# Two graph layers on one core: doubly buffered probabilities, the output written per head by VectorE, the probabilities' residual on GpSimd

## The reference

```python
# layer 0: W1 = W2 = adj
h = jnp.maximum(_layernorm(x), 0.0)
A = einsum('od,bdn->bon', adj, h);  C = A + b
x = x + max over the last axis of relu(A[:, :, None, :] + (C - A)[:, :, :, None])
# layer 1: masked attention, 8 heads of 64
h = jnp.maximum(_layernorm(x), 0.0)      # the kernel folds both norms into one h
q, k, v = h @ Wq + bq, h @ Wk + bk, h @ Wv + bv
scores = q k^T / 8 + (-1e9 where adj == 0)
x = x + softmax(scores) @ v
```

## Time and profile before

| | |
|---|---|
| median of 3 runs | 1403.61 us (1401.77 to 1403.91) |
| the profiled execution | 1401.24 us |
| its span, first to last instruction | 1399.4 us |
| mean granted clock of TensorE | 0.977 of full |
| PE busy | 1310.5 us, 94% |
| POOL busy | 1251.0 us, 89% |
| DVE busy | 1125.2 us, 80% |
| ACT busy | 878.7 us, 63% |
| chain that ended last | PE 55%, DMA 22% (nearly all probsT<-probs), DVE 15% |

### The profile page before, as it was taken

One profiled execution on the slowest core, in us unless ns is written; L12 is line 12 of the kernel. 1 busy time (PEld: TensorE's weight loads), 2 busy tenths in 40 slices (PEclk: granted clock), 3 DMA queues, 4 the chain that ended last, 5 costly groups with the idle time before them and its releaser, 6 DMA issues.

```text
span 1399.4 us, 32539 instructions
## 1 busy us (share of the span) xinstructions
PE 1310.5 (94%) x11145; PEld 657.2 (47%) x11145; DVE 1125.2 (80%) x1460; ACT 878.7 (63%) x1294; POOL 1251.0 (89%) x1288
## 2 busy tenths in 40 slices
PE   4899999999999999999999999999999999999962
PEld 1344444444444444454445444444444444444531
DVE  6468878888888788788898888888789888887874
ACT  4666666666666666666666666666666666666531
POOL 2889999999999999999999999999999999999721
PEclk8999999999999999999999999999999999999975
DMA  6235554555545545556455554655545556555534
GB/s 197 60 84 107 136 129 114 138 123 123 139 113 132 130 113 140 123 123 139 112 137 126 125 137 112 137 125 124 136 115 135 128 120 140 115 134 114 90 78 104
DMA packets 441372, 171.66 MB, mean 123 GB/s; under 512 B 406784, under 2 KB 406912, under 8 KB 441344
## 3 DMA queue, kind: packets, MB, share of 16 engines
q1 hardware_dynamic: 440000, 171.03, 52.7%
q10 hardware_dynamic: 1344, 0.27, 0.1%
HBM read 37.03 MB, written 33.55 MB: 50 GB/s over the span
## 4 chain that ended last, share of the span: by engine, by line
PE 55%; DMA 22%; DVE 15%; issue 4%; SPq 2%; ACT 1%; DVEq 0%; POOL 0%; POOLq 0%; ACTq 0%
PE proj L691 26%; DMA probsT<-probs 21%; PE proj L703 13%; PE o_ps L735 7%; DVE probs L495 7%; PE proj L676 6%; PE sc L720 4%; DVE attn L527 3%; SPq L239 2%; DVE a_max L481 1%; DVE out_scale L523 1%; DVE mean_var L474 1%; DVE inv_sum L521 1%; DMA x_in<-in_x 0%; SPq L219 0%
## 5 line engine op out<-in xcount | busy, mean ns | idle before, releaser
L691 PE MATMUL proj<-hT,w 128*128 128x512 f16 x3072 | 688.4, 381 | 11.5 <-DMA hT<-h 7.1
L691 PEld LDWEIGHTS proj<-hT,w 128*128 128x128 f16 x3072 | 291.0, 98 | 360.3 <-issue 16.8
L703 PE MATMUL proj<-w,hT 128*128 128x512 f16 x1536 | 352.4, 379 | 1.1 <-DVE w L579 1.1
L339 POOL TENSOR_TENSOR qkT<-qk,qkT 128x512 f16<-128x512 f32 x256 | 298.6, 1167 | 12.1 <-ACT qk L392 11.9
L407 ACT ACTIVATE probs<-shifted 128x1024 f16<-128x1024 f32 x128 | 135.3, 1057 | 193.7 <-DMA probsT<-probs 180.3
L390 ACT ACTIVATE qkT<-proj,bqk_up 128x512 f16<-128x512 f32 x256 | 173.4, 677 | 108.3 <-PE proj L691 108.3
L481 DVE TENSOR_REDUCE a_max<-proj 128x1 f32<-128x512 f32 x124 | 85.8, 692 | 191.5 <-PE proj L676 191.3
L327 POOL TENSOR_TENSOR xbv<-x_in,bv_rows 128x512 f32<-128x512 f32 x128 | 227.6, 1778 | 10.6 <-POOL y L318 2.2
L703 PEld LDWEIGHTS proj<-w,hT 128*128 128x128 f16 x1536 | 149.9, 98 | 181.6 <-DVE w L579 1.5
L511 DVE TENSOR_TENSOR shifted<-masked,row_max 128x1024 f32<-128x1024 f32 x128 | 210.7, 1646 | 13.4 <-ACT probs L409 9.1
L318 POOL TENSOR_TENSOR y<-attn,x 128x512 f32<-128x512 f32 x128 | 162.6, 1271 | 48.6 <-DVE attn L527 48.6
(11 more groups left out here) (61 smaller groups left out, 1125.2 us busy)
## 6 DMA issues: line engine op xcount, KB each, us to landing
x_in<-in_x SPq DMA_DIRECT2D x128, 256.0 KB, 2.9
out_x<-y SPq DMA_DIRECT2D x128, 256.0 KB, 2.2
hT<-h SPq DMA_TRANSPOSE x128, 3.1
probsT<-probs SPq DMA_TRANSPOSE x128, 4.4
w_raw<-in_L_gnn_Wq SPq DMA_DIRECT2D x1, 1024.0 KB, 9.0
w_raw<-in_L_gnn_Wv SPq DMA_DIRECT2D x1, 1024.0 KB, 11.3
w_raw<-in_L_gnn_Wk SPq DMA_DIRECT2D x1, 1024.0 KB, 13.4
bv_rows<-in_L_gnn_bv ACTq DMA_DIRECT2D x1, 256.0 KB, 6.7
```

Source lines behind the costliest of these rows:

```text
L339: pool.tensor_tensor(qk_place(k, u, 1), qk32[:, u % 2, :], qk_place(k, u, 0), ALU.subtract).then_inc(qk_rest_done, 1)
L691: last = nc.tensor.matmul(proj[:, u % 2, :], w16[:, j, s, c, col * P:(col + 1) * P], hT[:, k // GROUP % 2, t, c, :, :].rearrange("p g n -> ...
L703: last = nc.tensor.matmul(proj[:, V_BANK, :], hT[:, k // GROUP % 2, s, c, k % GROUP, :], w16[:, 2, t, c, :], start=(c == 0 and i == 0), st ...
```

## The change

- probs16 and probsT get a second buffer, chosen by the parity of the graph; `probsT_done` becomes two semaphores. `exps` of a graph waits for the transpose of two graphs before.
- `probs_rest` moves from DVE to POOL, in all slots and the tail, between `norm_scales` and the second `qk_rest`.
- `finish` on POOL and the tensor attn go. `attention_out` on DVE writes y itself, with eight instructions (one per head, 64 columns): output in PSUM times out_scale plus x1. It moves from graph k-6 to k-7 and to just behind the moments' wait; the semaphore o_evac is gone, y_done takes its place.
- DVE's slot is now `softmax_shift`(k-5), `adjacency_out`(k+3), `v_rest`, `stats_of`, `attention_out`(k-7), `moments_of`.
- PE's slot is now `scores`, `qk_chunk` twice, `adjacency`, `v_rows`, `probs_times_v`.
- `add_c` and `c_of` handle graph k instead of k+1.
- SP: load (waiting for x1_done), transposition of h, store, transposition of the probabilities, with the same waits in the loop as outside.
- The tail uses three pairs of PSUM banks for the scores instead of two.

```diff
-LOAD_AHEAD, MOMENTS_AHEAD, NORM_AHEAD, TURN_AHEAD, PREP_AHEAD, X1_AHEAD = 8, 6, 5, 5, 4, 1
+LOAD_AHEAD, MOMENTS_AHEAD, NORM_AHEAD, TURN_AHEAD, PREP_AHEAD, AMAX_AHEAD = 8, 6, 5, 5, 4, 3
+V_BEHIND, Y_BEHIND = 1, 7
-        probs16 = sb("probs16", [P, 2, H, P], F16)
-        probsT = sb("probsT", [P, 2, H, P], F16)
+        probs16 = sb("probs16", [P, 2, 2, H, P], F16)
+        probsT = sb("probsT", [P, 2, 2, H, P], F16)
-        attn = sb("attn", [P, 2, D])
-        pairs_of_banks = (sc, proj[:, 0:2, :])
+        TAIL_BANKS = (sc, proj[:, 0:2, :], proj[:, 2:4, :])
...
             def transpose_probs(base, k):
                 if in_range(base, k):
+                    sp.wait_ge(probs_rest_done, base + k + 1)
+                    wait(sp, o_ready, base + k - 1)
...
             def slot(base, k):
-                if isinstance(base, int):
-                    load(base, k + LOAD_AHEAD)
-                else:
-                    sp.wait_ge(o_evac, base + k - OUT_BEHIND + 1)
-                    sp.dma_start(x_in[:, k % RING, :], x[base + k + LOAD_AHEAD, :, :]).then_inc(x_loaded[k % RING], 16)
-                transpose_probs(base, k - ATTN_BEHIND)
+                load(base, k + LOAD_AHEAD)
                 transpose(base, k + TURN_AHEAD)
                 store(base, k - STORE_BEHIND)
+                transpose_probs(base, k - ATTN_BEHIND)
...
+            def probs_rest(base, k):
+                if in_range(base, k):
+                    pool.wait_ge(probs_head_done, base + k + 1)
+                    pool.wait_ge(probs_done, base + k + 1)
+                    pool.tensor_tensor(probs16[:, k % 2, 1, :, :], probs[:, :, :], probs16[:, k % 2, 0, :, :],
+                                       ALU.subtract).then_inc(probs_rest_done, 1)
...
             def slot(base, k):
                 u = 2 * (k % GROUP)
-                add_c(base, k + X1_AHEAD)
+                add_c(base, k)
                 rest(base, k + NORM_AHEAD)
                 qk_rest(base, k, u)
                 norm_scales(base, k + MOMENTS_AHEAD)
+                probs_rest(base, k - ATTN_BEHIND)
                 qk_rest(base, k, u + 1)
-                finish(base, k - OUT_BEHIND)
...
-                    wait(act, probsT_done, m * 16)
+                    wait(act, probsT_done[k % 2], (m - k % 2) * 8)
...
-                    wait(dve, y_done, m - 1)
-                    nc.vector.tensor_tensor(attn[:, k % 2, :].rearrange("p (t h d) -> p t h d", t=2, d=HD),
-                                            o_view[:, :, :, 0:HD],
-                                            out_scale[:, :, :].unsqueeze(3).to_broadcast([P, 2, H // 2, HD]),
-                                            ALU.mult).then_inc(o_evac, 1)
+                    dve.wait_ge(x1_done, m + 1)
+                    wait(dve, y_stored[k % 2], (m - k % 2) * 8)
+                    for h in range(H):
+                        cols = slice(h * HD, h * HD + HD)
+                        last = nc.vector.scalar_tensor_tensor(y[:, k % 2, cols], o_view[:, h // 4, h % 4, 0:HD],
+                                                              out_scale[:, h // 4, h % 4:h % 4 + 1],
+                                                              x1[:, k % RING, cols], ALU.mult, ALU.add)
+                    last.then_inc(y_done, 1)
...
             def slot(base, k):
                 softmax_shift(base, k - ATTN_BEHIND)
-                v_rest(base, k - 1)
+                if not isinstance(base, int) or base + k > 0:
+                    adjacency_out(base, k + AMAX_AHEAD)
+                v_rest(base, k - V_BEHIND)
                 stats_of(base, k + MOMENTS_AHEAD)
                 moments_wait(base, k + MOMENTS_AHEAD)
-                adjacency_out(base, k + PREP_AHEAD)
+                attention_out(base, k - Y_BEHIND)
                 moments_of(base, k + MOMENTS_AHEAD)
-                probs_rest(base, k - ATTN_BEHIND)
-                attention_out(base, k - OUT_BEHIND)
...
-                    wait(pe, o_evac, m)
+                    wait(pe, y_done, m)
...
                 qk_chunk(base, k, u + 1)
-                probs_times_v(base, k - OUT_BEHIND)
                 adjacency(base, k + PREP_AHEAD)
                 v_rows(base, k)
+                probs_times_v(base, k - OUT_BEHIND)
```

More of the change, by code:

```diff
@@ L154, in graph_layers @@
             sem("s_ready"), sem("masked_done"), sem("max_done"), sem("shifted_done"), sem("probs_done"))
[L155 to L157 removed]
+        probs_head_done, probs_rest_done = sem("probs_head_done"), sem("probs_rest_done")
+        probsT_done = [sem(f"probsT_done{i}") for i in range(2)]
+        o_ready, inv_sum_done, out_scale_done, y_done = sem("o_ready"), sem("inv_sum_done"), sem("out_scale_done"), sem("y_done")
+        c_done, xc_done, x1_done = sem("c_done"), sem("xc_done"), sem("x1_done")
         def wait(eng, s, count):
@@ L218, in transpose @@
                 if in_range(base, k):
+                    m = base + k
+                    sp.wait_ge(h_rest_done, m + 1)
+                    wait(sp, qk_ready, 2 * (m - m % GROUP - GROUP))
+                    wait(sp, v_ready, m + 1 - 2 * GROUP)
                     sp.dma_start_transpose(
@@ L309, in rest @@
                                        ALU.subtract).then_inc(h_rest_done, 1)
[L311 to L319, removed]
             def add_c(base, k):
@@ L358, in slot @@
                 norm_scales(base, k + MOMENTS_AHEAD)
+                probs_rest(base, k - ATTN_BEHIND)
                 qk_rest(base, k, u + 1)
-                finish(base, k - OUT_BEHIND)
             slots(pool, slot)
-            for k in range(-OUT_BEHIND, 0):
-                finish(B, k)
+            for graph in TAIL:
+                probs_rest(*graph)
         @block.scalar
@@ L480, in adjacency_out @@
                     wait(dve, c_done, m - RING + 1)
-                    nc.vector.tensor_reduce(a_max[:, k % RING, :], proj[:, A_BANK, :], AX.X, ALU.max).then_inc(a_evac, 1)
+                    rows = FIRST_BANKS[k] if isinstance(base, int) and m < PREP_AHEAD else proj[:, A_BANK, :]
+                    nc.vector.tensor_reduce(a_max[:, k % RING, :], rows, AX.X, ALU.max).then_inc(a_evac, 1)
             def v_rest(base, k):
@@ L647, in slot @@
                 softmax_shift(base, k - ATTN_BEHIND)
-                v_rest(base, k - 1)
+                if not isinstance(base, int) or base + k > 0:
+                    adjacency_out(base, k + AMAX_AHEAD)
+                v_rest(base, k - V_BEHIND)
                 stats_of(base, k + MOMENTS_AHEAD)
                 moments_wait(base, k + MOMENTS_AHEAD)
-                adjacency_out(base, k + PREP_AHEAD)
+                attention_out(base, k - Y_BEHIND)
                 moments_of(base, k + MOMENTS_AHEAD)
-                probs_rest(base, k - ATTN_BEHIND)
-                attention_out(base, k - OUT_BEHIND)
             slots(dve, slot, after_first=k_rest)
-            v_rest(B, -1)
-            softmax_shift(*TAIL[0], pairs_of_banks[0])
-            for i, (base, k) in enumerate(TAIL):
-                if i + 1 < len(TAIL):
-                    softmax_shift(*TAIL[i + 1], pairs_of_banks[(i + 1) % 2])
-                probs_rest(base, k)
-                attention_out(base, k - 1)
-            attention_out(*TAIL[-1])
+            v_rest(B, -V_BEHIND)
+            for i, graph in enumerate(TAIL):
+                softmax_shift(*graph, TAIL_BANKS[i % 3])
+                attention_out(B, graph[1] - Y_BEHIND + ATTN_BEHIND)
+            for k in range(-Y_BEHIND + ATTN_BEHIND, 0):
+                attention_out(B, k)
         @block.tensor
@@ L734, in probs_times_v @@
                             w = HD if t else VW
-                            last = nc.tensor.matmul(o_view[:, h // 4, h % 4, 0:w], probsT[:, s, h % 2 * 4 + h // 2, :],
+                            last = nc.tensor.matmul(o_view[:, h // 4, h % 4, 0:w], probsT[:, k % 2, s, h % 2 * 4 + h // 2, :],
                                                     v16[:, t, k // GROUP % 2, k % GROUP, h, 0:w],
```

55 lines of the change are left out of this document (16 added, 39 removed).

## The result

The changed kernel takes **1387.03 us** (median of 4 runs, 1386.83 to 1387.11) against 1403.61: a ratio of 0.9884 [0.9867, 0.9902]. It is faster by 16.6 us, or 1.2%: half of the 32.6 forecast. The profiled execution took 1386.83 us, with a span of 1384.9 against 1399.4.

A forecast was written before the change was run, and what follows sets the result against it. GpSimd was taken to bound the kernel, though TensorE's busy share was higher. From the profiled 1401.2 us, 18.6 in the loop and 12 in the tail were subtracted: 1370.6, so 1371 us, range 1355 to 1397.

The forecast's parts named there:

- What bounded the kernel: In the loop GpSimd, which never stands still, sets the pace at 10.34 us a slot; ScalarE's 134.7 us wait costs nothing.
- GpSimd's sum: GpSimd's slot with the addition out, the residual in, one lock given back: 9.93 to 10.28 us, taken as 10.15.
- The lock of L511: VectorE's shifted row and GpSimd's two-SBUF-input operations exclude one another; it stays, costing GpSimd 0.86 to 0.98 us.
- The tail: Five graphs after the last slot: two buffers open the serial circle, VectorE paces at 5.8 us per graph; 12 us saved.
- The output rows: VectorE's eight output instructions on 64 columns, 0.21 us each, take 1.1 us; bounds 0.7 and 2.2.
- a slack of 1.2: VectorE's chain ends at 8.1 us, TensorE asks at 9.30: 1.2 us to pay waits behind GpSimd.
- I add 0.03 us: Allowance per loop slot after finding the slacks just used up by VectorE's waits; the slot is taken as 10.18 us.
- rival (b): Loop keeps its pace: residual 2.3 us, L523 locks each time, slot 10.3 to 10.4; 1385 to 1400 us; chance 0.24.
- loop term: Loop slots fall to 10.18 us, 0.16 saved each, times 116: 18.6 us.
- Rival (c): New circle: GpSimd's norm_scales waits for VectorE's mean_var behind the output; slot 10.8 to 10.9, 1449 us; chance 0.10.
- Rival (a): The loop reaches TensorE's floor of 10.03 us per slot: 1353 us; chance 0.17.
- Rival (d): The move loads GpSimd and no lock is given back, +0.72 us per slot: 1473 us; chance 0.03.

The follow-up runs named there:

- e1: Changed kernel with inv_sum placed in PSUM, so out_scale reads from there; all else stays: 1363.19 us, 0.9715.
- e9: Changed kernel with the eight output instructions made one row of 512 columns, the addition of x1 left out: 1358.47 us, 0.9684.
- e8: Changed kernel with inv_sum in PSUM and the probabilities' residual back on VectorE in the slots (the tail's stay on GpSimd): 1354.58 us, 0.966.
- e2: Changed kernel with rounds of 16 slots instead of 8 in the hardware loop, otherwise the same: 1431.27 us, 1.0205.
- e3: Kernel before, with GpSimd's addition y cut to one column and the output stored from attn, without x1: 1375.75 us, 0.9813.

## Why the prediction was half right

**What bounded the kernel** was read rightly. GpSimd set the pace, ScalarE's long wait did not: shown by the run without the addition and the run with the double buffer alone.

**GpSimd's sum** was right. The residual takes 2.136 us (forecast 2.11), var_eps 0.189 with its lock gone, and the slot about 10.1 (forecast 10.15). e1 turns this into a measured pace, 10.107, and a time of 1363 where GpSimd's sum decides. The lock of L511 on the GpSimd row beside it is in the new kernel too: xbv, 1.26 where nothing held it, has a mean of 2.25 over the 116 slots, 0.99 more; 0.86 to 0.98 was forecast. Its group in the changed kernel, 97 to 1294 us (busy us, mean ns):

```profile
L277 POOL TENSOR_TENSOR xbv<-x_in,bv_rows 128x512 f32<-128x512 f32 x116 | 261.0, 2250 | 0.0
```

**The tail** was right: 12.3 against 12, the last probs x V of the five at 1378.7-1341.6 = 37.1 us behind the last scores, against 36.6.

**The output rows** were undersized. Eight rows of 0.21 with a step of 0.13 were to take 1.1 us; they take 0.276 each, a step of 0.193, 1.63 in all. The bound given as the upper one, 0.27 a row, was the right length; the fixed part was chosen from a difference of two long rows (0.08) when the short row L523 (0.20) was the nearer one. That took 0.5 us from a slack of 1.2. It also decides what a lost race costs: with 1.1 us TensorE would have stood about 0.4 us (0.91-0.53) instead of 0.91. This is an estimate from the rows above; the run with 0.69 us (e9) supports it, and none has 1.1.

**"I add 0.03 us"** is the step that failed: what TensorE loses behind the waits of VectorE. They were priced by L511's, as half an operation on average, and the slack as just used up, so that little was left over. But in this loop out_scale's wait has two values, 0 and 0.93 us, decided by less than 0.2 us between two starts. Where it is 0, TensorE doesn't wait; where it is 0.93, y comes 0.9 us too late, the whole slot is late by that, and GpSimd loses 0.83 for mean_var. An average put against a slack hides this: the mean loss over eight slots, 0.29 us above the floor (2.3/8), comes from two of them. The forecast had 0.15.

**The rivals.** The time is that of rival (b), 1385 to 1400, and its loop's "10.3 to 10.4" is met, but its reasons weren't: the residual didn't cost 2.3, and L523 (L467 in the changed kernel) locked in 33 slots, not in each. That 1387 also lies inside the stated range of 1355 to 1397 is no merit of the sum, whose loop term gave 18.6 us where 3.7 came. Rival (c)'s circle, GpSimd waiting for mean_var, is there (21.9 us), as a consequence of lost races and not as a pace of its own. Rival (a), the floor, is what e8 reaches, 1354.6 against its 1353. Rival (d) is refuted: var_eps' lock was given back.

**What stays open.** Why inv_sum comes 0.1 to 0.2 us later in the first slots of a round is not explained; the profile names stats, VectorE's own row ahead of it, as releaser. That the edge is the place is shown (e2, and every round of the changed kernel); which of the edge's instructions delays it isn't. Open too are what holds the loop at 10.13 without GpSimd's addition (e3), and which part of the change took the transposes off the chain.

## What to carry to other kernels

Ask which engine never waits before believing a large wait elsewhere: 134.7 us of ScalarE's waiting were worth nothing in the loop. Price a wait for another engine's running operation by the two start times: write down the lead, what is left of the operation if it is lost, and what each outcome does to the next deadline; don't set half an operation against a slack. A tiny row on the path, with all its operands in SBUF and a long GpSimd operation beside it, is worth a place in PSUM for its operand; here that one line brought 24 us, more than the whole change. And try it before moving large work between engines: with the lock in place the residual on GpSimd saves 49 us (1435.8 against 1387.0), without it it costs 8.6.

## What the runs showed of the hardware

- A VectorE row of 8 columns with one SBUF tensor as input (and a scalar per partition) is excluded by a running GpSimd operation with two inputs as a large one is: 0.23 us becomes 1.08 to 1.20 when it comes just behind the operation's start, and 0.37 to 0.93 when less of it is left. With its tensor in PSUM it is 0.224 to 0.228 in all 128 cases, in two kernels. The Trainium skill, GPSIMD Engine Reference, Specifications, names contention for VectorE instructions with two SBUF inputs or in a 2-port mode. This row has one such input; that it runs in a 2-port mode no run here shows. The trace agrees as to the contention, with the waits above, each to the end of the running operation.
- A start 0.13 us ahead of the GpSimd operation escapes it; one 0.02 to 0.05 behind waits 0.9 us, and so does one that is recorded 0.01 ahead (697.22 against 697.23).
- Eight VectorE rows of 64 columns from PSUM with a scalar per partition step by 0.193 us and last 0.276 each, 1.63 in all; one row of 512 columns takes 0.69.
- A hardware loop with a body of 16 slots instead of 8 raised the packets of the instruction queue from 16 to 106 and cost 11 to 12 us at each edge.
